# Selective-scan block of a two-layer tower: 64x64 drive tiles, a logarithm added by TensorE, and gates shared by two engines

## The reference, cut to what matters

```python
proj = hidden_states @ W_in.T
u, gate = jnp.split(proj, 2, axis=-1)
...
u = jax.nn.silu(jnp.transpose(x, (0, 2, 1)) + conv_b)
ssm_p = u @ Wx.T
dt, Bm, Cm = jnp.split(ssm_p, [R, R + N], axis=-1)
...
delta = jax.nn.softplus(dt @ Wdt.T + dt_bias)

def step(state, xs):
    d_t, B_t, C_t, u_t = xs
    dA = jnp.exp(d_t[..., None] * A)
    state = dA * state + (d_t * u_t)[..., None] * B_t[:, None, :]
    y_t = jnp.einsum('bdn,bn->bd', state, C_t)
    return (state, y_t)
...
y = jnp.swapaxes(ys, 0, 1) + u * D_param
y = y * jax.nn.silu(gate)
return y @ W_out.T
```

## Time and profile before

| | us |
|---|---|
| median of 3 runs | 4074.54 |
| lowest and highest | 4069.95, 4077.92 |
| the profiled execution, its own time | 4075.14 |
| its span in the profile | 4073.3 |
| scan stretch of the first block, first scan to last scan's end | 704.3 to 1028.8 |
| busy over the span: PE / DVE / ACT / POOL | 3868.0 / 2674.6 / 2057.9 / 2235.6 |

### The profile page before, as it was taken

The page is one execution under the profiler, slowest core; times in us unless marked ns, Lnnn a source line. Parts: engine busy times, 40 slices in busy tenths (PEclk is TensorE's granted clock), DMA queues, the critical chain, the costliest instruction groups (busy, mean ns, idle before and its releaser), DMA issues.

```text
span 4073.3 us, 59277 instructions
## 1 busy us (share of the span) xinstructions
PE 3868.0 (95%) x22816; PEld 2542.0 (62%) x22816; DVE 2674.6 (66%) x2922; ACT 2057.9 (51%) x3012; POOL 2235.6 (55%) x972
## 2 busy tenths in 40 slices
PE   4899999999999999999999999999999999999998
PEld 1568777444678777544577877644377877744466
DVE  6965562999356563799635565499835557299943
ACT  7842344777232343777433233577633234477732
POOL 0023343999533343799733434599943443389952
PEclk7999999999999999999999999999999999999999
DMA  4242234000322224200132223400132223400022
GB/s 113 78 145 83 83 113 158 10 16 15 116 99 84 73 92 153 71 16 16 66 108 99 83 68 122 143 13 16 40 109 99 78 88 104 157 29 16 15 85 73
DMA packets 96697, 320.18 MB, mean 79 GB/s; under 512 B 12353, under 2 KB 16705, under 8 KB 91841
## 3 DMA queue, kind: packets, MB, share of 16 engines
q1 hardware_dynamic: 80320, 275.70, 20.6%
q10 hardware_dynamic: 16128, 41.03, 3.0%
HBM read 272.51 MB, written 44.17 MB: 78 GB/s over the span
## 4 chain that ended last, share of the span: by engine, by line
PE 35%; issue 32%; DVE 20%; POOL 11%; ACT 1%; POOLq 0%; ACTq 0%; DVEq 0%
PE psg L947 20%; DVE sb_wst L1746 17%; POOL sb_wl L522 9%; PE psx L1198 4%; PE psg L1017 3%; POOL sb_wst L561 2%; PE psg L1214 2%; PE psg L1022 1%; PE psx L1246 1%; DVE psg L1719 1%; DVE psg L1718 1%; PE psg L1317 1%; PE psx L964 0%; PE psg L1173 0%; DVE sb_rt L1834 0%
## 5 line engine op out<-in xcount | busy, mean ns | idle before, releaser
L522 POOL TENSOR_TENSOR sb_wl<-sb_raw,sb_wh 128x1024 fp32r<-128x1024 f32 x388 | 959.1, 2476 | 1760.0 <-ACT sb_wh L642 1759.7
L1746 DVE TENSOR_TENSOR_SCAN sb_wst<-sb_dA,psx 128x1024 f32<-128x1024 f32 x512 | 1130.2, 2268 | 9.4 <-PE psx L1198 7.4
L642 ACT ACTIVATE sb_wh<-sb_raw 128x1024 fp32r<-128x1024 f32 x388 | 407.5, 1053 | 558.7 <-PE psg L947 227.6
L784 ACT ACTIVATE sb_dA<-sb_dlt,sb_a_sb 128x504 f32<-128x504 f32 x1024 | 647.0, 705 | 51.8 <-DVE sb_wst L1746 49.6
L1198 PEld LDWEIGHTS psx<-sb_dgB,sb_duT 64*128 64x128 f32 x4096 | 360.4, 188 | 462.5 <-DVE sb_wst L1746 323.4
L1198 PE MATMUL psx<-sb_dgB,sb_duT 64*128 64x256 f32 x4096 | 587.4, 406 | 51.0 <-DVE sb_wst L1746 49.4
L1214 PE MATMUL psg<-sb_wst,sb_cst 64*64 64x512 f32 x4096 | 611.6, 623 | 17.3 <-POOL sb_wst L561 16.4
L561 POOL TENSOR_TENSOR sb_wst<-sb_wst,sb_cb_hi 128x1024 f32<-128x1024 f32 x256 | 596.1, 2362 | 29.9 <-DVE sb_wst L1746 29.5
L561 POOL TENSOR_TENSOR sb_wst<-sb_wst,sb_cb_lo 128x1024 f32<-128x1024 f32 x256 | 600.7, 2371 | 10.6 <-DVE sb_wst L1746 10.2
L947 PE MATMUL psg<-sb_xh,sb_wh 128*128 128x512 f32 x2080 | 532.1, 398 | 12.6 <-POOL sb_wl L522 7.1
L947 PE MATMUL psg<-sb_xh,sb_wl 128*128 128x512 f32 x2080 | 515.6, 390 | 0.0
(11 more groups left out here) (274 smaller groups left out, 4959.8 us busy)
## 6 DMA issues: line engine op xcount, KB each, us to landing
sb_raw<-in_w SPq DMA_DIRECT2D x360, 512.0 KB, 3.5
sb_raw<-w_ffn_dequantized SPq DMA_DIRECT2D x32, 512.0 KB, 3.3
gates<-sb_gt ACTq DMA_DIRECT2D x64, 256.0 KB, 2.2
sb_gin<-gates SPq DMA_DIRECT2D x64, 256.0 KB, 2.7
h_after_tok<-sb_h SPq DMA_DIRECT2D x4, 2048.0 KB, 8.9
sb_cb_lo<-c_rows ACTq DMA_DIRECT2D x8, 1024.0 KB, 6.3
sb_cb_hi<-c_rows ACTq DMA_DIRECT2D x8, 1024.0 KB, 7.4
sb_h<-h_after_tok SPq DMA_DIRECT2D x4, 2048.0 KB, 7.7
```

Source lines behind the costliest of these rows:

```text
L522: pool.tensor_tensor(rest(b, i0), raw[:, i0 % RAW, :, :], high(b, i0).bitcast(F32), ALU.subtract).then_inc(s_wl, 1)
L642: A(high(b, i0), raw[:, i0 % RAW, :, :], ACT.Copy).then_inc(s_wh, 1)
L784: ins_ = A(dA[:, (m * NQ + k) % RING, :, n, 1:S], dlt[:, m % 2, :].rearrange("p (b s) -> p b s", b=NB)[:, :, 1:S], ACT.Exp, scale=a_sb[:, ...
L1746: v.tensor_tensor_scan(wst[:, x, 4 * j:4 * j + 4, :, :].rearrange("p b n s -> p (b n s)"), dA[:, x, 4 * j:4 * j + 4, :, :].rearrange("p b ...
```

## The change: what it does

- `drives` writes each product as two, one for each half of the output partitions: eight products of 64 rows by 64 columns in place of four of 64 by 128, with the same moving operand.
- DVE's addition of the logarithm (L1728) goes. A new PE routine `logarithm(m)` adds `spt` onto bank 2 by one float32 product with the 128x128 identity, 512 moving columns, accumulating. It waits for `soft_sum` and for ACT's logarithm. It stands after strip 10 of the gate for chunk 0, and at g = 2, behind the sums, for the others. `drive_sum` waits for it. The wait between DVE's L1719 and its own next instruction goes too, since no DVE instruction needs it any more.
- Odd chunks are gated by DVE from PSUM (L1735's form), at g = 6 of the chunk behind, for m = 1, 3, ..., 13 (and 15 as before); ACT no longer copies them out (`summed`), POOL gates the even ones alone. The semaphores are split: `s_y` counts even, `s_yo` odd chunks.
- `drive_sum(0)` moves from gate strip 9 to gate strip 10 on DVE.

```diff
@@ SP
-                        sp.wait_ge(s_y, b * DC + m - 1 + CR_Y)
+                        if m >= 2 and m % 2 == 0:
+                            sp.wait_ge(s_y, b * (DC // 2) + m // 2)
+                        if m >= 2 and m % 2 == 1:
+                            sp.wait_ge(s_yo, b * (DC // 2) + m // 2)
@@ POOL
-                            if g == 1 and m >= 2:
+                            if g == 1 and m >= 2 and m % 2 == 0:
                                 gated(m - 2)
@@ ACT
-                            if m >= 1:
+                            if m % 2 == 1:
                                 summed(m - 1)
...
-                    act.wait_ge(s_y, (b + 1) * DC + CR_Y)
+                    act.wait_ge(s_y, (b + 1) * (DC // 2))
+                    act.wait_ge(s_yo, (b + 1) * (DC // 2))
@@ PE, delta
                         if m >= 3:
-                            pe.wait_ge(s_yc, b * (DC - 1) + m - 2)
+                            if m % 2 == 1:
+                                pe.wait_ge(s_yc, b * (DC // 2) + (m - 3) // 2 + 1)
+                            else:
+                                pe.wait_ge(s_yo, b * (DC // 2) + (m - 4) // 2 + 1)
@@ PE
+                    def logarithm(m):
+
+                        pe.wait_ge(s_own["sp"], b * 2 * DC + 2 * m + 2)
+                        pe.wait_ge(s_sp2, b * DC + m + 1)
+                        pe.matmul(psg[:, 2, :], C("ident"), spt[:, 0, :], start=False, stop=True,
+                                  skip_group_check=True).then_inc(s_ln, 1)
@@ PE, drives
-                            for r in range(2):
-                                r0 = 64 * r
-                                ins_ = mm(psx[:, 2 * j + r, :].rearrange("p (a t e) -> p a t e", a=8, e=2)[:, :, :, e],
-                                          duT[r0:r0 + 64, m % 2, i * P:(i + 1) * P],
-                                          dgB[r0:r0 + 64, i, k, :, :, :], start=True, stop=True)
+                            for c in range(2):
+                                for r in range(2):
+                                    r0 = 64 * r
+                                    ins_ = mm(psx[64 * c:64 * c + 64, 2 * j + r, :].rearrange("p (a t e) -> p a t e", a=8, e=2)[:, :, :, e],
+                                              duT[r0:r0 + 64, m % 2, i * P + 64 * c:i * P + 64 * c + 64],
+                                              dgB[r0:r0 + 64, i, k, :, :, :], start=True, stop=True)
@@ PE, gate strips
+                        if m == 10:
+                            logarithm(0)
@@ PE, scan stretch
                             sums_due(m * G + g - 3)
+                            if g == 2 and m < DC - 1:
+                                logarithm(m + 1)
@@ DVE
                     def soft_sum(m):
...
                         own.link(stt(x, spt[:, 1, :], 1.0, x, ALU.subtract, ALU.subtract))
-                        own.link(tt(x, dlt[:, m % 2, :], x, ALU.subtract))
+                        tt(x, dlt[:, m % 2, :], x, ALU.subtract).then_inc(s_own["sp"], 1)
 
                     def drive_sum(m):
...
-                        v.wait_ge(s_sp2, b * DC + m + 1)
+                        v.wait_ge(s_ln, b * DC + m + 1)
                         if m >= 1:
                             v.wait_ge(s_tr, b * DC + m)
-                        own.link(tt(x, spt[:, 0, :], x, ALU.add))
                         tt(du[:, :], x, u[:, m, :], ALU.mult).then_inc(s_dlt, 1)
@@ DVE, scan stretch
+                            if g == 6 and m >= 2 and m % 2 == 0:
+                                gated(m - 1)
```

More of the change, by code:

```diff
@@ L344, in tower @@
         s_zr = sem("s_zr")
+        s_ln = sem("s_ln")
+        s_yo = sem("s_yo")
         s_yh, s_yl = sem("s_yh"), sem("s_yl")
@@ L549, in gated @@
                     def gated(m):
-                        pool.wait_ge(s_yc, b * (DC - 1) + m + 1)
+                        pool.wait_ge(s_yc, b * (DC // 2) + m // 2 + 1)
                         pool.wait_ge(s_gin[m % 2], 16 * (b * (DC // 2) + m // 2 + 1))
@@ L1293, in _ @@
                         sums_due(step)
-                    pe.wait_ge(s_yc, b * (DC - 1) + DC - 1)
+                    pe.wait_ge(s_yc, b * (DC // 2) + DC // 2)
                     finals(DC - 1, False)
@@ L1383, in _ @@
             v.sem_inc(s_scan, CR_SCAN)
-            v.sem_inc(s_y, CR_Y)
             v.wait_ge(s_mode, 80)
@@ L1715, in soft_sum @@
                         x = psg[:, 2, :]
-                        own = Own(v, s_own["sp"], b * 3 * DC + m * 3)
+                        own = Own(v, s_own["sp"], b * 2 * DC + m * 2)
                         v.wait_ge(s_sp1, b * DC + m + 1)
                         own.link(stt(x, spt[:, 1, :], 1.0, x, ALU.subtract, ALU.subtract))
-                        own.link(tt(x, dlt[:, m % 2, :], x, ALU.subtract))
+                        tt(x, dlt[:, m % 2, :], x, ALU.subtract).then_inc(s_own["sp"], 1)
                     def drive_sum(m):
                         x = psg[:, 2, :]
-                        own = Own(v, s_own["sp"], b * 3 * DC + m * 3 + 2)
-                        v.wait_ge(s_sp2, b * DC + m + 1)
+                        v.wait_ge(s_ln, b * DC + m + 1)
                         if m >= 1:
                             v.wait_ge(s_tr, b * DC + m)
-                        own.link(tt(x, spt[:, 0, :], x, ALU.add))
                         tt(du[:, :], x, u[:, m, :], ALU.mult).then_inc(s_dlt, 1)
@@ L1734, in gated @@
                         v.wait_ge(s_gin[m % 2], 16 * (b * (DC // 2) + m // 2 + 1))
-                        tt(u[:, m, :], psg[:, 2, :], gin[:, m % 2, :], ALU.mult).then_inc(s_y, 1)
+                        tt(u[:, m, :], psg[:, 2, :], gin[:, m % 2, :], ALU.mult).then_inc(s_yo, 1)
                     def scan(m, g):
```

## The result

| | before | after |
|---|---|---|
| median, us | 4074.58 (4 runs, 4069.95 to 4077.92) | 4037.43 (4 runs, 4036.44 to 4038.09) |
| ratio to before | 1 | 0.9906, 95% interval 0.9894 to 0.9918 |
| profiled execution / its span | 4075.14 / 4073.3 | 4036.44 / 4034.4 |

What follows compares the result with a forecast made beforehand. DVE was taken as the bound of the scan stretch. Per block -8.2 - 1.2 - 0.8 + 1.0 + 0.5 = -8.7, four blocks -35, from 4075.1 to 4040 us; range 4025 to 4060.

Steps and rivals of the forecast that it cites:

- DVE's terms: DVE in the scan stretch: logarithm 10.65 and a wait 1.8 saved, seven gates 4.3 added; net 8.2 us less per block.
- the link: DVE's wait between L1719 and its next instruction: removing it saves 0.12 us each, 15 times per block, 1.8.
- PE's terms: PE per chunk: 64x64 drives save 2.1 us (step 2.08 to 1.82), the logarithm adds 1.0; 19.80 becomes 18.7.
- rival A: Drives don't get shorter and PE becomes the bound: 4108 us, or near 4185 if each half costs more; chance 0.07.
- The tight place: PE's drives for scan 6, behind transposes and finals, come just in time: 0.03 us stall a chunk, 0.5 more per block.
- Nothing is late behind it: PE's logarithm, placed after the u * D products, delays neither the next drives nor DVE's du.
- The first chunks: DVE's waits of 0.32 and 0.45 us for drives in the first block go: 0.8 less per block.
- POOL's end: POOL's last work after the last scan no longer includes chunk 13's gate: 1.2 us less per block.
- The good side: Block's end: POOL ending earlier shortens PE's 2.66 pause by about 1.2; clock kept up saves 1.4 to 2; not counted.
- C: POOL becomes the pacemaker through hidden waits, or the gate waits for finals or its load: 4070 us; chance 0.05.
- B: DVE newly waits on drives, 0.1 to 0.4 us idle per chunk, eating the gain: 4046 to 4064; chance 0.12.
- chunk 0: PE's logarithm for the first chunk stands among the gate strips, where PE runs without pause: 1.0 us more per block.

Runs made afterwards that it cites:

- e2: Kernel before with the 64x64 drives alone, nothing else changed: 4074.38 us, ratio 0.9997.
- e4: Changed kernel with the logarithm added by DVE again, with its wait, so only tiles and gates differ from the kernel before: 4080.84 us, ratio 1.0013.
- e1: Changed kernel with its drives put back to four products of 64 by 128: 4097.88 us, ratio 1.0051.
- e5: Changed kernel with PE also adding the softplus's linear part by a second identity product, ACT making -(1 + e), DVE's soft_sum one instruction: 4049.34 us.
- e3: Changed kernel with the gates of all chunks but the last back on POOL: 4048.52 us, ratio 0.9933.
- e10: e5 with the finals moved behind the drives for scan 6 in PE's queue (g = 4 to g = 5): 4017.25 us, ratio 0.9857.
- e7: Changed kernel with products nobody reads placed in PE's pauses at a block's end: 4028.47 us, ratio 0.988.

## Why the prediction was right

**What bounds it.** DVE, by the rows of a chunk, though three engines lay within 3% of each other. Shown by e2 (PE relieved, POOL untouched: nothing to be measured) and e4 (DVE loaded again: the whole gain gone). The signs that the prediction named came out too: DVE 99% busy in chunks of 19.35 and 19.95, the weight loads ahead of their matmuls, and in the odd chunk two gaps of POOL of 0.54 and 0.26, together the 0.8.

**DVE's terms.** -8.2 forecast, -8.8 measured (-11.0 - 1.95 + 4.2). The distance of two starts in one row's neighbourhood was the right unit: 0.71 for the logarithm came out as 0.73, the link's 0.12 as 0.13, a gate's 0.61 as 0.60 from chunk to chunk.

**PE's terms.** A step of 1.82 was forecast; it is 1.72 where PE doesn't wait (twice 0.86). That is 0.36 saved in place of 0.26, so twice 0.18 for the two changes of shape that went, in the upper part of the 0.1 to 0.2. The logarithm's 1.0 is 1.19 from start to next start, of which a part may be the wait for a scan; in e1, where PE never waits, it is 1.06. PE's chunk came out at 18.9 and 19.2 busy where 18.7 stood; I take it that merged rows with waits between them count more, which no run shows by itself. What was said against rival A held: 16 records of drives need no more than 0.86.

**The tight place.** Forecast at 0.03 of stall a chunk (the forecast's own sum, 4.87 against 4.89, would have given none), found at none. But it is a true limit: e5 put 0.96 ahead of it, asked for the scan 0.72 earlier, and DVE lost 0.92 a chunk. "Nothing is late behind it", said of the logarithm, holds for one product and not for two.

**The first chunks.** Mis-sized: -1.5 for -0.8. I had counted the two waits of the earlier trace rows and not looked at the last chunk, where DVE waited another 0.52; and in the first chunk more than the wait shown went.

**POOL's end.** Mis-sized: -0.75 for -1.2. POOL runs without a gap up to its last product, and the scans now end earlier too, by the 0.52 of DVE's lost wait; the lag behind them can't shrink by the whole gate. That the difference of 0.45 is this was read, not tried.

**The good side.** Wrong. I held that POOL's earlier end would shorten PE's pause of 2.66 and perhaps keep the clock up. The pause is 2.66 again: it is the length of POOL's last two products (1021.34 - 1016.74 = 4.60) less PE's own sums of 1.95, and has nothing to do with when POOL ends. The low clock at the ends of the four blocks cost 1.7 more than before, 0.4 a block, with one block better and one much worse. It was left out of the sum. Since it comes out differently from block to block under the same pauses, I don't take the 1.7 for a property of the change.

**The rivals.** A is what e1 shows, at 4098, not 4108 to 4185: 0.47 over today's chunk, not 0.57. B appears in e5. C appears in e3, and no worse than 4048.5: even a POOL without any gap only starts to brake after some four chunks.

So 4040 against 4037.4 is in part luck. Over the four blocks of the two traces, the stretches gave 8 more than forecast (42.2 for 34: DVE's prices, the waits and the tight place were all taken too cautiously), and chunk 0 cost 0.6 less. Against that, POOL's end gave 1.9 less, the clock took 1.7, and 1.1 went outside the scan layers. What is left is 4 us more gained than forecast in the two traces (38.9 for 34.8), and 2.4 more in the medians.

## What to carry to other kernels

Where several engines are within a few per cent of each other, the gain of an edit is not additive: price it on every one of them, and expect that a part by itself may be worth nothing (the tiles) or less (the logarithm without the tiles, 21 us slower than before). Before adding work to an engine with room in its sum, look at the one place in its order that the bound engine waits for soonest; a product of 1 us there cost more than it saved (e5), and moving one block of work behind that place gave 32 us (e10). An engine that falls behind by little in each chunk may show it only at the end of the stage (e3), so look at the last chunk before comparing steady ones. The pauses of PE at the end of a stage can be paid twice, in the pause and in the clock of what follows; filling them brought 9 us (e7).
